# A graph layer on one core: six selected tiles in one chunk of five, and a rearranged end

## The reference

```python
h  = relu(layernorm(x))
xl = einsum('ni,nio->no', h, hetero_w[node_type]) + hetero_b[node_type]
ete = leaky(edge_type_emb[edge_type])              # 16 per edge
eae = leaky(edge_attr @ edge_attr_w)               # 16 per edge
alpha = leaky(concat([xl[dst], xl[src], ete, eae]) @ att_w)
alpha = exp(alpha - segment_max(alpha, dst)[dst])
alpha = alpha / (segment_sum(alpha, dst)[dst] + 1e-16)
msg = concat([xl[src], eae]) @ lin_w * alpha
out = x + segment_sum(msg, dst)
```

## Time and profile before

| What | us |
|---|---|
| profiled execution, its own time | 3413.38 |
| its span in the trace | 3411.6 |
| TensorE matmul busy | 3067.4 (90%) |
| TensorE weight loads busy (beside the matmuls) | 2610.0 (77%) |
| VectorE busy | 2951.0 (86%) |
| GpSimd (POOL) busy | 2495.9 (73%) |
| ScalarE busy | 900.4 (26%) |

### The profile page before, as it was taken

The page is one execution under the profiler, slowest core; times in us unless marked ns, Lnnn a source line. Parts: engine busy times, 40 slices in busy tenths (PEclk is TensorE's granted clock), DMA queues, the critical chain, the costliest instruction groups (busy, mean ns, idle before and its releaser), DMA issues.

```text
span 3411.6 us, 66571 instructions
## 1 busy us (share of the span) xinstructions
PE 3067.4 (90%) x21488; PEld 2610.0 (77%) x21488; DVE 2951.0 (86%) x7241; ACT 900.4 (26%) x2094; POOL 2495.9 (73%) x2629
## 2 busy tenths in 40 slices
PE   7799999999999999999999999999999999999900
PEld 6688888878878888888888888888887887887700
DVE  6799999889889888988989889888988988998835
ACT  3223232223222232222323223232222222222200
POOL 2577777777777777777777777777777777777656
PEclk6799999999999999999999999999999999999955
DMA  3433333333333333333333333333333333336322
GB/s 119 117 73 91 72 91 72 91 72 86 77 72 91 72 88 76 79 85 72 91 72 83 80 72 91 72 88 78 76 89 72 91 72 73 91 72 153 74 74 73
DMA packets 186011, 284.37 MB, mean 83 GB/s; under 512 B 73954, under 2 KB 140986, under 8 KB 185212
## 3 DMA queue, kind: packets, MB, share of 16 engines
q1 hardware_dynamic: 76796, 165.55, 16.1%
q0 software_dynamic: 84768, 52.50, 13.0%
q10 hardware_dynamic: 24288, 64.79, 5.3%
HBM read 210.13 MB, written 72.48 MB: 83 GB/s over the span
## 4 chain that ended last, share of the span: by engine, by line
DVE 28%; PE 27%; POOL 23%; issue 17%; DMA 4%; DVEq 0%; POOLq 0%; ACT 0%; SPq 0%; ACTq 0%
POOL gath L598 20%; PE ps_misc L834 19%; DVE sel_a L1150 10%; DMA gath<-table_dram,meta 4%; DVE sel_b L1150 4%; DVE gath L1164 3%; PE ps_pick L848 3%; DVE dscore L1172 3%; DVE slot_a L1152 1%; PE ps_misc L836 1%; DVE ps_msg L1241 1%; PE ps_misc L804 1%; POOL hib L639 1%; DVE ps_misc L1211 1%; PE ps_attr L858 1%
## 5 line engine op out<-in xcount | busy, mean ns | idle before, releaser
L598 POOL DMA_INDIRECT gath<-table_dram,meta x2500 | 2364.3, 946 | 831.8 <-issue 733.3
L834 PE MATMUL ps_misc<-parts,sel_a 128*128 128x462 f32 x5250 | 1219.0, 383 | 94.3 <-DVE gath L1164 94.1
L834 PEld LDWEIGHTS ps_misc<-parts,sel_a 128*128 128x128 f32 x5250 | 973.9, 191 | 220.6 <-DVE gath L1164 120.4
L834 PE MATMUL ps_misc<-parts,sel_b 128*128 128x462 f32 x3500 | 806.5, 381 | 28.4 <-DVE gath L1164 25.0
L834 PEld LDWEIGHTS ps_misc<-parts,sel_b 128*128 128x128 f32 x3500 | 644.9, 189 | 117.8 <-DVE gath L1164 43.6
L848 PE MATMUL ps_pick<-s_dst,onehot 122*128 122x128 bf16 x9375 | 652.4, 220 | 29.6 <-DVE s_dst L1304 14.2
L848 PEld LDWEIGHTS ps_pick<-s_dst,onehot 122*128 122x128 bf16 x9375 | 540.0, 98 | 172.9 <-issue 126.2
L1172 DVE TENSOR_REDUCE dscore<-ps_pick 128x4 f32<-128x512 f32 x875 | 521.5, 618 | 1.2 <-PE ps_pick L848 1.1
L1164 DVE TENSOR_REDUCE gath<-ps_misc 128x33 f32<-128x462 f32 x625 | 391.9, 627 | 142.3 <-PE ps_misc L836 142.3
L728 ACT ACTIVATE wts<-args 128x50 f32<-128x50 f32 x125 | 30.8, 246 | 1680.5 <-DVE args L1263 1680.5
L1150 DVE TENSOR_SCALAR sel_a<-dst_f,part_group 128x384 fp32r<-128x384 f16 x875 | 465.4, 604 | 0.0
(11 more groups left out here) (239 smaller groups left out, 1933.5 us busy)
## 6 DMA issues: line engine op xcount, KB each, us to landing
hib<-digit_dram SPq DMA_DIRECT2D x125, 612.5 KB
rows_dram<-rows ACTq DMA_DIRECT2D x125, 437.5 KB, 5.0
gath<-table_dram,meta POOLq DMA_INDIRECT x2500
attr<-edge_attr_t_in SPq DMA_DIRECT2D x125, 200.0 KB
dst_f<-sel_code_dram SPq DMA_DIRECT2D x125, 160.0 KB
hib<-digit_dram SPq DMA_DIRECT2D x250, 50.0 KB
rows_dram<-no_rows ACTq DMA_DIRECT2D x1, 8575.0 KB, 44.5
hib<-digit_dram SPq DMA_DIRECT2D x250, 25.0 KB
```

What stands on the lines that cost most here:

```text
L598: nc.gpsimd.indirect_dma_start(gath[u][:, t, :], None, table_dram, bass.IndirectOffsetOnAxis(ap=meta_sb[u][:, t:t + 1], axis=0)).then_inc( ...
L834: nc.tensor.matmul(ps_sel, rows_of[:, g, at, 0:P], parts[:, k, g, :], start=(g == 0 and k == 0), stop=False)
```

## The change

The third chunk of a round selects six tiles and gathers 19; the other four stay at five and 20. The sixth tile stands in `sel_b` and `slot_b`, which now have room for three, and so do the code tables (750 instead of 625 columns) and their loads (768 instead of 640). TensorE's last round is written out behind its loop, now of 24 rounds, so that the final chunk can have its own number of selected tiles (`TS_LAST`, five here); the count of falls (L905) moves ahead of the last count of signs. At the end the tails are read from the last `rows` buffer in SBUF instead of memory, the flag is read before the wait for the stored rows, the load of `x_end` is issued as soon as the last selection is done, and the "own" gather no longer waits for `head_idx_ready`. In the last stage one operand of the marking, multiplying and averaging instructions lies in PSUM (`node_of`, `is_last`, `inverse`, `averaged`), and the last group of nine is split into six and three, with an output of its own each.

```diff
-TS = 5
+TS_OF = (5, 5, 6, 5, 5)
+TS = max(TS_OF)
 TS_A = 3
+TS_LAST = 5
...
+            (hib_sb[0][:].bitcast(fp32)[:, 6 * BLOCK * RW:9 * BLOCK * RW], 3),
+            (hib_sb[0][:].bitcast(fp32)[:, 0:6 * BLOCK * RW], 6),
...
+        is_last = [in_bank(ps_msg, 0, BLOCK * last_at[k], w, BLOCK) for k, (_, w) in enumerate(last_in_buf)]
+        inverse = ps_msg[:, 1, 0:NPP]
+        node_of = ps_msg[:, 1, NPP:2 * NPP]
+        averaged = ps_pick[:].rearrange("p a b -> p (a b)")
+        row_tails = rows[U - 1][:, T - 1, :]
...
+            sp.wait_ge(sel_mm, count(SELECTED))
+            sp.dma_start(x_end[:], x).then_inc(x_end_in, 16)
+            flag = is_unsorted(sp)
             for u in range(U):
                 sp.wait_ge(stored[u], 16 * ITERS + 1)
-            flag = is_unsorted(sp)
-            sp.wait_ge(sel_mm, count(CHUNKS * TS))
-            sp.dma_start(x_end[:], x).then_inc(x_end_in, 16)
-            with sp.If(flag < 1):
-                sp.dma_start(tails[:], rows_pm[:, EPP - 1, :]).then_inc(tails_in, 16)
-                sp.wait_ge(tails_in, 16)
...
+            flag = is_unsorted(pool)
             for u in range(U):
                 pool.wait_ge(stored[u], 16 * ITERS + 1)
-            flag = is_unsorted(pool)
             with pool.If(flag < 1):
-                pool.wait_ge(head_idx_ready, 1)
...
+            def chunk(i, u, final):
+                c = i * U + u
+                tiles = TS_LAST if final else TS_OF[u]
+                dst_scores(c, 0)
+                select(i, u, 0)
+                attr_product(i, u)
+                dst_scores(c, 1)
+                select(i, u, 1)
+                dst_scores(c, 2)
+                if tiles > 5:
+                    select(i, u, 2)
+                dst_scores(c, 3)
+                if 2 < tiles <= 5:
+                    select(i, u, 2)
+                if tiles > 5:
+                    select(i, u, 3)
+                dst_scores(c, 4)
+                messages(c)
+                if tiles > 3:
+                    select(i, u, tiles - 2)
+                dst_scores(c, 5)
+                dst_scores(c, 6)
+                if tiles > 3:
+                    select(i, u, tiles - 1)
+                if final:
+                    count_falls()
+                count_signs(c)
...
                     picks(front, 3)
                     if not last_front:
                         select_first(*later)
+                    if takes > 5:
+                        take(*after, 3)
                     picks(front, 4)
-                    take(*after, 3)
+                    if takes > 3:
+                        take(*after, takes - 2)
...
-                dve.wait_ge(tails_in, 16)
-                v.tensor_copy(mtail[:], tails[:, VW:VW + 1].broadcast_to([P, P])).then_inc(head_idx_ready, 1)
+                dve.wait_ge(rows_sums, count(CHUNKS))
+                v.tensor_copy(mtail[:], row_tails[:, VW:VW + 1].broadcast_to([P, P])).then_inc(head_idx_ready, 1)
...
                 finished(v.tensor_tensor(buf[:, :, :, 0:VW], buf[:, :, :, 0:VW],
-                                         is_last[:, n, :].unsqueeze(3).broadcast_to([P, w, BLOCK, VW]), ALU.mult))
+                                         is_last[k].unsqueeze(3).broadcast_to([P, w, BLOCK, VW]), ALU.mult))
```

More of the change, by code:

```diff
@@ L35, with turns @@
 SIGNS_AFTER = PICKS - 1
-TS = 5
+TS_OF = (5, 5, 6, 5, 5)
+TS = max(TS_OF)
 TS_A = 3
+TS_LAST = 5
 SEL = CHUNKS * TS
-GATHERED = T - TS
-TURNS = tuple(GATHERED * k // 5 for k in range(6))
+SELECTED = ITERS * sum(TS_OF) - TS_OF[-1] + TS_LAST
+def turns(n):
+    return tuple(n * k // 5 for k in range(6))
 HIB_OF = (0, 1, 2, 3, 1)
@@ L247, in gnn_kernel @@
         own = sb("own", [P, RW])
-        tails = sb("tails", [P, RW])
         contrib = sb("contrib", [P, P])
@@ L398, in selected @@
         def selected(i, u):
-            return (i * U + u) * TS
+            return i * sum(TS_OF) + sum(TS_OF[0:u])
         def start_at_one(eng, *sems):
@@ L596, in gather_chunk @@
                         pool.sem_inc(gather_turns, 1)
-                    for t in range(TURNS[k], TURNS[k + 1]):
+                    for t in range(turns(taken)[k], turns(taken)[k + 1]):
                         nc.gpsimd.indirect_dma_start(
@@ L602, in _ @@
             for u in range(U):
-                gather_chunk(0, u, u < AHEAD)
-            with pool.Fori(1, ITERS) as i:
+                gather_chunk(0, u, u < AHEAD, T - TS_OF[u])
+            with pool.Fori(1, ITERS - 1) as i:
                 for u in range(U):
-                    gather_chunk(i, u, False)
+                    gather_chunk(i, u, False, T - TS_OF[u])
+            for u in range(U):
+                gather_chunk(ITERS - 1, u, False, T - (TS_OF[u] if u < U - 1 else TS_LAST))
+            flag = is_unsorted(pool)
             for u in range(U):
                 pool.wait_ge(stored[u], 16 * ITERS + 1)
-            flag = is_unsorted(pool)
             with pool.If(flag < 1):
-                pool.wait_ge(head_idx_ready, 1)
                 nc.gpsimd.indirect_dma_start(own[:], None, rows_dram,
@@ L830, in select @@
                 rows_of, slots_of, at = (sel_a, slot_a, j) if j < TS_A else (sel_b, slot_b, j - TS_A)
-                pe.wait_ge(sel_read, count(c * TS + j))
+                pe.wait_ge(sel_read, count(selected(i, u) + j))
                 for g in range(NG):
@@ L903, in _, with count_falls @@
-            pe.wait_ge(falls_ready, 1)
-            pe.wait_ge(sel_read, count(CHUNKS * TS))
-            nc.tensor.matmul(ps_misc[:, 0, 0:1], before_me[:], falls[:, 0:1], start=True, stop=True).then_inc(
-                falls_mm, 1)
+            def count_falls():
+                pe.wait_ge(falls_ready, 1)
+                pe.wait_ge(sel_read, count(SELECTED))
+                nc.tensor.matmul(ps_misc[:, 0, 0:1], before_me[:], falls[:, 0:1], start=True, stop=True).then_inc(
+                    falls_mm, 1)
@@ L907, in _ @@
+            with pe.Fori(0, ITERS - 1) as i:
+                for u in range(U):
+                    chunk(i, u, False)
+            for u in range(U):
+                chunk(ITERS - 1, u, u == U - 1)
             pe.wait_ge(sign_parts_ready, 1)
@@ L914, in _ @@
             with pe.If(flag < 1):
-                pe.wait_ge(tails_in, 16)
+                pe.wait_ge(rows_sums, count(CHUNKS))
                 pe.wait_ge(head_idx_ready, 1)
@@ L920, in _ @@
                 pe.wait_ge(wtailT_sb, 1)
-                nc.tensor.matmul(ps_misc[:, 0, 2 * P:2 * P + VW], wtailT[:], tails[:, 0:VW], start=True,
+                nc.tensor.matmul(ps_misc[:, 0, 2 * P:2 * P + VW], wtailT[:], row_tails[:, 0:VW], start=True,
                                  stop=True).then_inc(tsum_mm, 1)
@@ L1230, in chunk @@
                 last_front = isinstance(i, int) and c + 2 >= CHUNKS
+                takes = TS_LAST if isinstance(i, int) and c + 2 == CHUNKS else TS_OF[after[1]]
                 if final:
@@ L1236, in chunk @@
                 sum_signs(c)
-                dve.wait_ge(gathered[u], (i + 1) * (16 * GATHERED))
+                if final:
+                    dve.wait_ge(gathered[u], 16 * ((T - TS_OF[u]) * ITERS + TS_OF[u] - TS_LAST))
+                    dve.wait_ge(sel_read, count(SELECTED))
+                else:
+                    dve.wait_ge(gathered[u], (i + 1) * (16 * (T - TS_OF[u])))
+                    dve.wait_ge(sel_read, count(selected(i, u) + TS_OF[u]))
                 dve.wait_ge(msg_mm, count(c + 1))
-                dve.wait_ge(sel_read, count(selected(i, u) + TS))
                 for part_of_it, tiles in msg_parts:
@@ L1244, in chunk @@
                 if not final:
-                    select_rest(*after)
+                    if takes > TS_A:
+                        select_rest(*after)
                     take(*after, 0)
@@ L1279, in chunk @@
                     attr_act(front)
-                    take(*after, 2)
+                    if takes > 2:
+                        take(*after, 2)
                     picks(front, 3)
@@ L1290, in chunk @@
                     penalties(after[1], at)
-                    take(*after, 4)
+                    if takes > 3:
+                        take(*after, takes - 1)
             for n in range(4):
@@ L1383, in _ @@
             v.tensor_copy(pos[:], cnt[:]).then_inc(pos_ready, 1)
+            finished = stage(last_step)
+            v.tensor_copy(node_of, node_id[:])
+            finished(v.memset(is_node, 0.0))
             flag = is_unsorted(dve)
```

54 lines of the change are left out of this document (21 added, 33 removed).

## The result

The changed kernel takes 3478.97 us (median of 4 runs, 3476.99 to 3484.23) where the kernel before takes 3417.87 beside it: a ratio of 1.0185, 95% interval 1.0165 to 1.0205. The forecast was 3452; the range ended at 3480.

The account below looks back on a forecast made before the run. GpSimd's gathers bound most of the loop; after the change TensorE and VectorE would. Loop +47.9, clock +12, join -7, marks -13, small last group -2 on 3413.4 gave 3451, forecast 3452; own range 3430 to 3475, quoted 3389 to 3480.

Parts of the forecast that it names:

- the sum for the loop: 124 chunk periods: TensorE and VectorE's own pace plus 25 longer third chunks, 3133.5 us, +47.9 on 3085.6.
- the 5.3 us of its own chunk: Third chunk of a round: growth from the sixth selection, 3.25 us of work and 2 of waiting.
- TensorE's exit: Unrolled last round on TensorE: costed at nothing; 2.6 us once if its exit were like VectorE's return.
- the 6.55: Loop's end: VectorE's 6.55 us wait for gathers, said to vanish with GpSimd ahead.
- the clock's 12 us: VectorE's loop returns: TensorE's clock falls to 1.2 GHz behind eight of 23, 1.55 us each, +12.
- the rival of a fall in every round: Loop: clock falls at the return and in the six-tile chunk, 74 us instead of 12; 3513, chance 0.09.
- the two named waits: Six-tile chunk: TensorE's selections 1 and 2 wait for VectorE's takes 0 and 1, 1.00 and 1.27 us.
- VectorE's delay was not absorbed: Six-tile chunk: the rival had the delay absorbed, growth only 3.25 us; 3401, or 3389 without clock losses; chance 0.11.
- marks: Last stage: operands in PSUM stop VectorE's long operations from lengthening GpSimd's gathers, -13 us.
- the rival that they buy nothing: Last stage: gathers stay as long with marks in PSUM, 13 us more, 3464; chance 0.07.
- the join's 7: Join after the loop: tails in SBUF let the "own" gather issue earlier, -7 us, between -6 and -7.2.
- rivals 3 and 4: Last stage: marks buy nothing, 3464, chance 0.07; loop: clock falls in every round, 3513, chance 0.09.

Follow-up runs that it names:

- run 2: The changed kernel with six tiles, but TensorE's last round not written out behind its loop, which runs 25 times: 3479.46 us.
- run 1: The changed kernel with five tiles selected and 20 gathers in every chunk, all other parts kept: 3400.96 us, ratio 0.994 to the kernel before.
- run 3: The changed kernel with five tiles in every chunk, plus four unneeded matmuls a chunk (20 a round) in TensorE's loop: 3400.61 us, ratio 0.994.
- run 5: The changed kernel with six tiles, TensorE's loop written over four rounds a trip: 3455.41 us, ratio 1.0119 to the kernel before.
- run 8: The changed kernel with five tiles in every chunk, the 8.6 MB write of empty rows issued in the middle of ScalarE's loop: 3396.08 us, ratio 0.9946.
- run 7: The changed kernel with five tiles in every chunk, the last stage's marks, inverse, node numbers and averages in SBUF again: ratio 0.9977 to the kernel before.
- run 11: The changed kernel with five tiles in every chunk, tails read back from DRAM and a last group of nine again: 3394.52 us, ratio 0.9943.
- run 6: The changed kernel with six tiles, TensorE's and VectorE's loops both written over four rounds a trip: 3401.36 us, ratio 0.9961.

## Why the prediction was wrong, step by step

**The step that failed** is the sum for the loop. It counts the returns of VectorE's loop and costs the sixth selection by the 5.3 us of its own chunk; a return of TensorE's loop stands in it at nothing. The prediction asked what TensorE's exit would cost once, for the unrolled last round (run 2 shows that this costs nothing), and never what 15 more matmuls do to TensorE's own return, 23 times: measured are 29.3 us of waiting there. The kernel before pays at two of 24 such returns, 3.8 us in all; that was the sign of how near the limit was, and the prediction didn't read it. Runs 1 and 3 show the cause with five tiles in both: 20 more matmuls in the loop bring the waits and the packets. Run 5 shows that it is the branch: with 5 returns the kernel takes 1.0119 of the time before, where the forecast was 1.0099.

The loop's 31.5 us over the forecast are, from the chunk periods of the one profile:
- the first chunks of 24 rounds, 25.05 for 23.7: +32.5 (29.3 of them in the "issue" row);
- the last four chunks 105.2 for 100.1: +5.1, the late signs and the clock at the loop's end, where the sum had put nothing in the place of the 6.55. It took that wait for GpSimd being just in time; by run 8 it goes with the write of the empty rows;
- the six-tile chunks 28.9 for 29.0: -2.2;
- the second chunks of rounds, with VectorE's return, 26.75 on average, forecast 26.72 with the clock's 12 us: +0.6. The clock fell behind 11 returns for 8; the rival of a fall in every round didn't come;
- the base: five chunks of 23.7 and a return of 2.5 are 121.0, where 121.2 was read from a window: -4.8 over the loop.

Together +31.2.

**What held.** GpSimd is no longer the bound (231.0 us of idle time beyond the issue of its gathers, 98.5 before), the six-tile chunk grows by 5.2 us through the two named waits (so VectorE's delay was not absorbed), VectorE's return is as before. The end: marks 12.9 for 13 (the rival that they buy nothing is out, run 7), small group 2.4 for 2. **Right size, wrong cause:** the join's 7; measured is 7.2 from store to first gather (20.3 to 13.1), but 5 of them came without the tails in SBUF (run 11). The remaining 2.3 come with the six-tile kernels: "own" is issued 3.4 us after the last store's issue in the changed kernel and in every run with a six-tile chunk, 5.6 to 5.8 in every run with none; why stays open.

The measured 3479 lies 4 us above the forecast's own range and 1 us inside the one quoted, through the room kept for rivals 3 and 4; neither came, so that it lies inside is luck.

Behind the chances: above 3452 stood only the marks, at 13 us, and the clock. A mechanism that costs a little at each of 23 returns was in the rows, for VectorE, and should have been a rival for TensorE, at 23 x 2.63 = 60 us at most: 3512.

## What to carry to other kernels

Before adding instructions to a loop, look at what its engine idles at a return ("issue" with no releaser) and at the packets of the instruction queue: a loop that returns for nothing can stop doing so with 2% more instructions, and the price is paid every trip. Writing several rounds into the body takes most of it away even though the code becomes longer. And when work is moved off the bound to an engine with 3.8 us to spare in a round, move only what fits: with both loops over four rounds, six tiles in 12 or 18 of the 125 chunks gave ratios of 0.987 to 0.989, in 25 of them 0.996; none at all, with one round a trip, gave 0.994.

## What the hardware showed

- TensorE's loop with 847 matmuls and as many weight loads a round returned for nothing at 22 of 24 returns before the change, and at 13 to 20 of 23 in the five-tile runs 1, 7, 8 and 11; with 862 (and with 867, run 3) it paid at every return, brought in 7.8 packets of 16.4 KB there and stood 0.6 to 1.8 us. The Trainium skill (Runtime: NRT & Kernel Launch, Instruction fetch mechanics) gives TensorE's instruction memory as 2048 instructions, refilled in blocks of 256, and says that a taken branch to a target outside a window of two pages stalls. The stall agrees, with 29.3 us in 23 returns. The sizes don't on their face: 847 pairs are 1694 instructions, far more than two blocks of 256, and mostly returned for nothing, and 862 pairs are 1724, with fewer than a hundred others in the loop still under 2048, and did not. The measured limit decides.
- The same section has the sequential fetch hidden; run 5 agrees, with 188 packets and 5.0 us of idle time.
- VectorE pays 2.4 to 2.9 us at every return of its loop in these kernels (6.8 at one, beside the moved write of run 8).
- TensorE and VectorE go on 1.4 to 1.9 us after a packet of instructions (q8 and q14) has landed, at every return at which they wait for it (kernel before, changed kernel, runs 3, 5 and 6).
